# A new beginning for a fused attention and FFN kernel: the order of its first loads, and the norm of tiles 8 to 31 turned to columns by DMA transposes

## The reference

```
normed = (x - mean) * rsqrt(var + 1e-5) * g + b
v, gate = split(silu(normed @ W_h + b_h))            # 2048 columns each
qk = silu(normed @ W_qk + b_qk)                      # 128 columns
quad_q, lin_q, quad_k, lin_k = qk * gamma[h] + beta[h]
per group of 256 tokens: attn = relu(quad_q @ quad_k.T / 256 + bias)**2
quad_out = attn @ v ;  lin_out = lin_q @ (sum over all tokens of lin_k.T @ v / 4096)
y = layernorm(x + (gate * (quad_out + lin_out)) @ W_o + b_o + x)
out = layernorm(y + relu(y @ W1 + b1) @ W2 + b2)
```

## Time and profile before

| | us |
|---|---|
| median of 3 runs | 1748.19 (1748.16 to 1748.96) |
| the profiled execution, its own time | 1749.52 |
| its span, core 0, first to last instruction | 1748.0 (other cores 1745.3 to 1747.4) |
| PE busy | 1703.2 |
| DVE, ACT, POOL busy | 548.0, 436.3, 316.4 |
| mean granted TensorE clock, core 0 | 0.994 |

### The profile page before, as it was taken

How to read it: one execution, slowest core, us unless ns; L and a number is a source line. 1 busy time by engine, 2 the same in 40 slices (tenths; PEclk the granted TensorE clock), 3 DMA queues, 4 the chain that set the end, 5 groups by cost and what they waited for, 6 DMA issues and landing times.

```text
span 1748.0 us, 23816 instructions; the slowest of 8 cores (1745.3 to 1748.0 us)
## 1 busy us (share of the span) xinstructions
PE 1703.2 (97%) x8320; PEld 805.3 (46%) x8320; DVE 548.0 (31%) x947; ACT 436.3 (25%) x684; POOL 316.4 (18%) x494
## 2 busy tenths in 40 slices
PE   3899999999999999999999999999999999999998
PEld 1344444445445445445444444444444444444443
DVE  3466654354454454454302012020120211202102
ACT  2344444312212213213230311303113022040220
POOL 3444442022322322312301001010010000100001
PEclk9899999999999999999999999999999999999999
DMA  7857762637467477454870112012220121110201
GB/s 176 181 141 187 190 166 79 175 112 155 141 164 152 143 169 144 144 139 123 191 217 37 61 37 84 12 44 67 37 63 22 49 73 37 50 36 25 73 1 48
DMA packets 93523, 180.94 MB, mean 104 GB/s; under 512 B 39648, under 2 KB 43744, under 8 KB 93408
## 3 DMA queue, kind: packets, MB, share of 16 engines
q1 hardware_dynamic: 78288, 149.77, 27.0%
q0 software_dynamic: 15120, 29.63, 12.5%
HBM read 139.53 MB, written 69.47 MB: 120 GB/s over the span
## 4 chain that ended last, share of the span: by engine, by line
PE 96%; DMA 1%; DVE 1%; POOL 1%; issue 1%; ACT 0%; SPq 0%; POOLq 0%; DVEq 0%; ACTq 0%
PE pb L725 25%; PE pb L702 25%; PE pb L668 13%; PE pb L634 13%; PE pb L569 12%; PE pb L656 3%; PE pb L650 2%; PE pb L579 2%; DMA xs<-x 1%; PE pb L539 1%; PE pb L550 1%; POOL n0s L451 0%; DVE nfm L815 0%; DVE bnst L227 0%; DVE bnst L228 0%
## 5 line engine op out<-in xcount | busy, mean ns | idle before, releaser
L702 PE MATMUL pb<-xfm,w1s 128*128 128x512 bf16 x2048 | 443.3, 379 | 0.0
L796 ACT ACTIVATE h<-pb,prms 128x512 bf16<-128x512 f32 x256 | 175.9, 687 | 653.2 <-PE pb L702 653.2
L702 PEld LDWEIGHTS pb<-xfm,w1s 128*128 128x128 bf16 x2048 | 200.4, 98 | 241.6
L929 DVE TENSOR_TENSOR xr<-pb,xr 128x512 f32<-128x512 f32 x64 | 44.2, 691 | 715.4 <-PE pb L725 715.4
L569 PE MATMUL pb<-wvs,nfm 128*128 128x512 bf16 x1024 | 248.8, 387 | 0.1
L634 PE MATMUL pb<-nfm,wgs 128*128 128x512 bf16 x1024 | 240.6, 379 | 0.0
L725 PE MATMUL pb<-w2a,h 128*128 128x512 bf16 x1024 | 231.5, 379 | 0.0
L668 PE MATMUL pb<-wos,gated 128*128 128x512 bf16 x1024 | 224.6, 379 | 0.0
L237 POOL TENSOR_SCALAR veps<-mv 128x1 f32<-128x1 f32 x96 | 21.8, 227 | 1002.2 <-DVE mv L232 1001.2
L725 PEld LDWEIGHTS pb<-w2a,h 128*128 128x128 bf16 x1024 | 100.2, 98 | 120.8
L569 PEld LDWEIGHTS pb<-wvs,nfm 128*128 128x128 bf16 x1024 | 100.3, 100 | 117.2 <-issue 12.9
(11 more groups left out here) (59 smaller groups left out, 1001.8 us busy)
## 6 DMA issues: line engine op xcount, KB each, us to landing
v_sp<-vst SPq DMA_DIRECT2D x32, 512.0 KB, 8.1
vb<-v_sp SPq DMA_DIRECT2D x32, 512.0 KB, 7.1
xr<-x SPq DMA_DIRECT2D x32, 512.0 KB, 13.1
x_sp<-xr SPq DMA_DIRECT2D x32, 512.0 KB, 3.0
xr<-x_sp SPq DMA_DIRECT2D x32, 512.0 KB, 8.0
out<-xr SPq DMA_DIRECT2D x32, 512.0 KB, 2.6
xt<-x SPq DMA_DIRECT2D x24, 512.0 KB, 5.7
w_sp<-w POOLq DMA_DIRECT2D x32, 256.0 KB, 13.8
```

The lines of the kernel that those rows point to most:

```text
L702: mm = te.matmul(pb[4 + n % 2][:], w1[:, w_:w_ + 128], xfm[:, x_:x_ + 512], start=(c == 0), stop=(c == 7))
L796: sc.activation(h1[:, ci * 512:(ci + 1) * 512], pb[4 + n % 2][:], AF.Relu, bias=prm[:, P_B1 + ci:P_B1 + ci + 1]).then_inc(S["s_h1"], 1)
```

## The change

First loads. SP issues x 0, x 1, prm (which now holds the identity as well), x 2, then Wv slice 0 as f32 in four parts of 512 KB into `wvf`, x 3, bv (now stored replicated for all partitions, in two parts), x 4, Wqk as f32 into `wqkf`, x 5 to x 7. ACT casts pieces 0 to 3 of slice 0 ahead of its first eviction, DVE pieces 4 to 7 behind its first. GpSimd loads slices 1 to 3 behind norm 2, 5 and 7. PE begins with 18 matmuls on zeros and has four more behind the transposes of tile 0.

Order. Units 4 to 11 alternate between slice 0 of tiles 4 to 7 and slice 1 of tiles 0 to 3. The statistics of tiles 3 to 7 stand at slots 0 to 4, those of a later tile at the slot of the columns of the tile before. Block 0's and block 1's qk stand at slots 5 and 11, their `lk_transpose` at 8 and 15, and GpSimd makes the heads of both behind norm 7.

Columns of tiles 8 to 31. PE's transposes and the evictions by ACT and DVE go. Instead SP issues a DMA transpose of the norm, SBUF to SBUF, for each tile (`columns`) at slots 14, 18, 22, 26, 30 and so on, and DVE applies g and b in place to the finished columns of a block (`affine`: eight operations of 128 x 512 bf16, four at slot 16b-3 and four at 16b-2). Norm t waits for the DMA transpose of tile t-2.

Smaller: GpSimd's -mean/std is split off `rs_chain` (`shift`) and left out in the last phase; bo and b2 are loaded from replicated arrays.

```diff
+GROUPS = ((0, 0), (1, 0), (0, 4), (1, 4), (2, 0), (2, 4), (3, 0), (3, 4))
+def place(u):
+    if 4 <= u < 12:
+        return 8 + (u - 4) // 2 - 4 * (u % 2)
+    return u
+def at_place(w):
+    if w < 32:
+        s, t0 = GROUPS[w // 4]
+        return t0 + w % 4, s
+    return w // 4, w % 4
...
+def store_slot(q):
+    return 13 if q == 1 else 4 * q + 5
 def t_slot(t):
     if t < 8:
-        return (0, 0, 0, 1, 2, 4, 5, 6)[t]
-    return 16 * (t // 4) - 15 + 4 * (t % 4)
+        return (0, 0, 1, 2, 3, 5, 7, 9)[t]
+    return 16 * (t // 4) - 18 + 4 * (t % 4)
 def stat_slot(t):
-    return (0, 1, 2, 3, 4, 8, 11, 14)[t - 3] if t < 11 else t_slot(t - 3)
+    return 4 + t if t < 11 else t_slot(t - 1)
+def aff_slot(b):
+    return 16 * b - 3
 def qk_slot(b):
-    return (3, 9)[b] if b < 2 else 16 * b
+    return (5, 11)[b] if b < 2 else 16 * b
 def lkt_slot(b):
-    return (7, 12)[b] if b < 2 else 16 * b + 4
+    return (8, 15)[b] if b < 2 else 16 * b + 4
...
# SP
         load_x_first(0)
+        load_x_first(1)
         sy.dma_start(out=prm[:], in_=prm_h[:, :]).then_inc(d_prm, 16)
-        sy.dma_start(out=ident[:], in_=id_h[:, :]).then_inc(d_id, 16)
-        load_x_first(1)
         load_x_first(2)
+        for c in range(4):
+            sy.dma_start(out=wvf[:, c * 1024:(c + 1) * 1024],
+                         in_=wv_h[0, :, c * 1024:(c + 1) * 1024]).then_inc(d_wvf[c], 16)
+        load_x_first(3)
         load_bv(0)
-        for t in range(3, 8):
+        load_x_first(4)
+        sy.dma_start(out=wqkf[:], in_=wqk_h[:, :]).then_inc(d_wqk, 16)
+        for t in range(5, 8):
             load_x_first(t)
+        load_bv(1)
...
+        def columns(t):
+            wt(sy, "s_n0", t + 1)
+            if t == 8:
+                wt(sy, "s_T", 8)
+            b, i = divmod(t, 4)
+            dst = nfm[:, b * 4096:(b + 1) * 4096].rearrange("p (c t) -> p c t", c=8)[:, :, i * 128:(i + 1) * 128]
+            sy.dma_start_transpose(out=dst, in_=n0_tile(t)).then_inc(d_T[t % 2], 16)
...
+        wt(sy, "s_n0", 6)
         load_x(8)
-        load_bv(1)
         load_x(9)
...
         for u in range(0, NU + 6):
-            for t in range(11, NT):
-                if ((10, 14)[t - 11] if t < 13 else t_slot(t - 5)) == u:
-                    load_x(t)
+            for t in range(8, NT):
+                if t_slot(t) == u:
+                    columns(t)
+                    if t + 3 < NT:
+                        load_x(t + 3)
...
# GpSimd
-        load_wv(0)
-        gp.dma_start(out=wqk[:], in_=wqk_h[:, :]).then_inc(d_wqk, 16)
...
             if t >= 10:
-                wt(gp, "s_T", t - 1)
+                wt(gp, d_T[t % 2], 16 * ((t - 8) // 2))
...
-            if t in (3, 5, 7):
-                load_wv((t - 1) // 2)
-            if t % 4 == 1 and t >= 5:
+            if t in (2, 5, 7):
+                load_wv(t // 2 if t < 7 else 3)
+            if t == 6:
+                head_lk(0)
+            if t == 7:
+                heads(0)
+                head_lk(1)
+                heads(1)
+            if t % 4 == 1 and t >= 13:
                 head_lk(t // 4 - 1)
-            if t % 4 == 1 and t >= 9 or t == 7:
-                heads(t // 4 - 1 if t > 7 else 0)
+                heads(t // 4 - 1)
...
# PE
+        def warm(n):
+            wt(te, "s_zero", 1)
+            for _ in range(n):
+                te.matmul(pb[3][:], vst[:, 0:128], vst[:, 128:640], start=True, stop=True)
...
         def v_unit(u):
...
             if s == 0:
-                wt(te, "s_nfa", t + 1)
-                wt(te, "s_nfd", t + 1)
+                wt(te, "s_nfa", min(t + 1, 8))
+                wt(te, "s_nfd", min(t + 1, 8))
+                wt(te, "s_aff", t // 4 - 1)
             wt(te, "s_vad", u - 1)
             for c in range(8):
+                if u == 0:
+                    wt(te, "s_wca", min(c + 1, 4))
+                    wt(te, "s_wcd", c - 3)
...
+        warm(18)
...
                 transposes(t)
+                if t == 0:
+                    warm(4)
...
# ACT
+        def cast_wv(c):
+            sc.wait_ge(d_wvf[c // 2], 16)
+            sc.copy(wv[:, c * 512:(c + 1) * 512], wvf[:, c * 512:(c + 1) * 512]).then_inc(S["s_wca"], 1)
+        for c in range(4):
+            cast_wv(c)
...
# DVE
+        def affine(b, half):
+            for i in range(2):
+                wt(ve, d_T[i], 16 * (2 * b - 2))
+            for c in range(4 * half, 4 * half + 4):
+                o_ = b * 4096 + c * 512
+                a = ve.tensor_scalar(nfm[:, o_:o_ + 512], nfm[:, o_:o_ + 512],
+                                     prm[:, P_NG + c:P_NG + c + 1], prm[:, P_NB + c:P_NB + c + 1],
+                                     ALU.mult, ALU.add)
+            if half:
+                a.then_inc(S["s_aff"], 1)
...
         for u in range(NU):
             for t in tiles_at(u):
                 nfm_evict(t)
-            for t in range(3, NT):
+                if t == 0:
+                    for c in range(4, 8):
+                        cast_wv(c)
+            if u < 5:
+                stats_a(u + 3)
+            for t in range(8, NT):
                 if stat_slot(t) == u:
                     stats_a(t)
+            for b in range(2, NB):
+                if u in (aff_slot(b), aff_slot(b) + 1):
+                    affine(b, u - aff_slot(b))
```

More of the change, by code:

```diff
@@ L73, in tiles_at @@
 def tiles_at(u):
-    return [t for t in range(NT) if t_slot(t) == u]
+    return [t for t in range(8) if t_slot(t) == u]
 def block_at(slot_of, u):
@@ L93, in build_program @@
     x_h = din("x", [NTOK, DM])
[L94 to L97, removed]
+    prm_h = din("prm", [128, P_N + 64])
+    bv_h = din("bv", [128, HID])
+    bo_h = din("bo", [128, DM])
+    b2_h = din("b2", [128, DM])
     wv_h = din("wv", [4, 128, 4096])
@@ L126, in build_program @@
     o = 131072
[L127 removed]
     biasT = at("biasT", o + 256, 512, F32)
[L129 removed]
+    prm = at("prms", o + 3072, P_N + 64, F32)
+    ident = prm[:, P_N:P_N + 64].bitcast(BF16)
     gs = at("gs", o + 2624, 4, F32)
@@ L447, in norm0 @@
             x_landed(gp, t)
+            shift(gp, t)
             wt(gp, "s_nm", t + 1)
             if t >= 10:
-                wt(gp, "s_T", t - 1)
-            gp.tensor_scalar(n0_tile(t), x_tile(t),
-                             rstd[:, j:j + 1], nmr[:, j:j + 1], ALU.mult, ALU.add).then_inc(S["s_n0"], 1)
+                wt(gp, d_T[t % 2], 16 * ((t - 8) // 2))
+            gp.tensor_scalar(n0_tile(t), x_tile(t), rstd[:, j:j + 1], nmr[:, j:j + 1],
+                             ALU.mult, ALU.add).then_inc(S["s_n0"], 1)
         def head_lk(b):
@@ L518, in emit_gpsimd @@
                 i = t % 4
+                if t >= 8:
+                    wt(gp, "s_x2f", t - 7)
+                shift(gp, NT + t)
                 if t == 0:
@@ L556, in lk_transpose @@
             for i in range(4):
-                mm = te.transpose(pT[:, i * 128:(i + 1) * 128], lkfm[:, i * 128:(i + 1) * 128], ident[:])
+                mm = te.transpose(pT[:, i * 128:(i + 1) * 128], lkfm[:, i * 128:(i + 1) * 128], ident)
             mm.then_inc(S["s_lkT"], 1)
@@ L748, in emit_scalar @@
                 wt(sc, "s_hd", b)
-                sc.activation(qkf[:], pb[7][:], AF.Silu, bias=prm[:, P_BQK:P_BQK + 1]).then_inc(S["s_qks"], 1)
-            q, j = divmod(u, 4)
+                sc.activation(qkf[:], pb[0 if b == 0 else 7][:], AF.Silu, bias=prm[:, P_BQK:P_BQK + 1]).then_inc(S["s_qks"], 1)
+            q, j = divmod(place(u), 4)
             if j == 0 and q >= 3:
@@ L833, in attn, with cast_wv @@
             ve.scalar_tensor_tensor(attnT[:, a_:a_ + 512], sims[:], 0.0, sims[:], ALU.max, ALU.mult).then_inc(S["s_att"], 1)
-        for t in range(3):
-            stats_a(t)
-            if t == 0:
-                scale_heads()
+        def cast_wv(c):
+            ve.wait_ge(d_wvf[c // 2], 16)
+            ve.tensor_copy(wv[:, c * 512:(c + 1) * 512], wvf[:, c * 512:(c + 1) * 512]).then_inc(S["s_wcd"], 1)
+        ve.memset(vst[:, 0:640], 0.0).then_inc(S["s_zero"], 1)
+        stats_a(0)
+        stats_a(1)
+        scale_heads()
+        stats_a(2)
         for u in range(NU):
@@ L1006 @@
         a["L0_ffn_b1"].reshape(32, 128).T,
+        np.eye(128, dtype=ml_dtypes.bfloat16).view(np.float32),
     ], axis=1)
```

106 lines of the change are left out of this document (59 added, 47 removed).

## The result

The changed kernel takes 1735.09 us (median of 4 runs, 1734.67 to 1738.21), the one before 1748.18 (1748.04 to 1748.96) in the same session: ratio 0.9928, 95% interval 0.9911 to 0.9945. That is 13.1 us faster, where the prediction said 28.2. The range (1709 to 1738) holds it only because its upper end was set past rival B; the gain itself missed by 15.1 us. In some executions the cores of one die show a lower granted clock and the time is longer; every time given here is a median of the other executions.

A forecast was written before the change was run, and what follows sets the result against it. PE, busy 97%, was taken to bound the kernel, so only its idle or half-speed stretches and work taken off it count: 22.6 + 10.6 - 3 - 2 = 28.2 us from 1749.5 gives 1721.3, so 1720 for the median; range 1709 to 1738.

The forecast's parts named there:

- rival B: Blocks' columns: they land late in each block, 3 us over the need x 6 = 18 instead of 2; 1736, chance 0.12.
- Transposes off PE: Tiles 8 to 31: 24 transposes of 0.44 us leave PE, with no stall hiding them; gain 10.6 us.
- The beginning: Up to V unit 21: the new load order cuts the loss from 47.6 to 25 us; gain 22.6, bounds 15.6 and 30.
- I take 25: New beginning: us still lost, a little over the sum of 22.5, since a first order loses something unseen.
- 0.36 MB/us: First loads on SP: assumed transfer rate, putting x 1 at 6.4 and Wv's four parts at 9.7 to 14.1 us.
- the 47.6 lost: Old beginning: V unit 21's start at 95.0 less 47.4 us of PE work done by then.
- x 5 after 32 us: Beginning: named sign that the forecast is wrong; x 5 was let land at 28 us.
- rival A: Beginning: bound by transfers, x 5 to x 7 and Wv slice 1 late; gain 11 instead of 22.6, 1732, chance 0.13.
- `affine`: 3 said: Slots 16b-2 of five blocks: DVE's added work stalls PE 0.4 to 1.4 us each, 2 to 7 in all, 3 taken.
- Lateness of the columns: 2 said: DMA transposes of six blocks: mostly no wait, 0 to 3 us each, 2 us taken in all.
- 7.2 us from issue, 8.5 to the need: Tile 4b+3's DMA transpose: lands 7.2 us after SP can issue it, while DVE needs it at 8.5.
- Rival C: SBUF transposes: one tile takes more than the 7.8 us four units leave, 23 us per us over; 1765, chance 0.10.

The follow-up runs named there:

- free_columns: Changed kernel with a 32-byte-a-partition copy in place of each DMA transpose, affine reading block 0, output wrong: 1726.27 us, 0.9873.
- pe_columns3: Changed kernel with columns of tiles 8 to 31 back on PE, ACT and DVE, block 0's qk waiting for its own four tiles: 1736.94 us, 0.9932.
- after: The changed kernel itself, against the kernel before: 1735.09 us, 0.9928; run again in another session 1739.93, 0.995.
- plain_copy: Changed kernel with each DMA transpose replaced by an untransposed copy of the same bytes in 256-byte pieces, output wrong: 1727.21 us, 0.9879.
- wv1_behind_3: Changed kernel with the casting load of Wv slice 1 behind norm 3 instead of norm 2: 1736.97 us, 0.9935.
- plain_loads: Changed kernel with Wg and Wo casting loads from tile 15 on, plus eight unused plain 512 KB loads behind norms 8 to 15: 1742.67 us, 0.9961.
- affine_later: Changed kernel with affine one slot later, at 16b-2 and 16b-1: 1749.83 us, 1.0005.

## Why the prediction was wrong

The runs split the change: 1748.2 before; 1736.9 with the new beginning alone; 1726.3 with columns for free; 1735.1 with the real transposes (from three groups, the middle two known to about 3 us by their intervals). So -11.3, -10.7 and +8.8 in place of -22.6, -10.6 + 3 and +2 (3 being `affine`, 2 the late DMAs).

**Transposes off PE: right.** 10.6 said, 10.7 measured with `affine` included. The traces agree: from V unit 21 to stage 2 the mean core takes 229.9 us before and 220.6 in `free_columns`, 9.3 less for 22 of the 24 tiles, 9.7 by the prediction's 0.44.

**The beginning: the step that failed.** "I take 25" for what the beginning loses; by the prediction's own count (the work done by unit 21 is 0.9 less) it lost 78.7 - 46.5 = 32.2 us on the mean core, from 93.6 - 47.4 = 46.2: 14.0 gained at that point, 11.3 at the end in `pe_columns3`. Two inputs were off. First, the rate: 0.36 MB/us was read from the slices from 17.5 us on in the earlier trace rows, and the slow stretch ahead of them was put down wholly to GpSimd's casting loads. In after GpSimd issues its first load at 15.36 us. GB/s in 40 slices, 0 to 20 us, of after:

```profile
GB/s 0 0 0 0 82 164 287 369 287 229 172 115 163 284 303 254 333 270 172 147 180 221 238 328 352 336 352 295 287 246 303 336 311 336 393 442 426 377 393 270
```

And the windows: two of after, then one of before (the last two columns are DMA share and GB/s):

```profile
5.00:15.00 10.00, 5.16 (x24) 2.00 (x22) 5.96 (x21) 1.41 (x3) 6.34 (x12) 0.96 0.98 252
5.00:18.70 13.70, 6.33 (x33) 2.99 (x32) 6.72 (x23) 3.75 (x9) 8.01 (x14) 0.84 0.98 283
```

```profile
5.00:15.00 10.00, 1.01 (x8) 0.78 (x8) 1.92 (x11) 1.50 (x4) 2.24 (x4) 1.00 0.96 160
```

So without the casting loads the stretch is faster, 252 GB/s instead of 160, but with engines as full it still dips (115 near 5.5 us, 147 near 9.5) and isn't at 360. x 1 came 2.9 us after x 0 and x 2 3.0 after that, 0.17 MB/us; x 1 to the last part of Wv, 3 MB, took 18.7 - 5.0 = 13.7 us, 0.22 MB/us. In these 13.7 us the engines moved 3.9 million bytes, and these six transfers are 3.15 million, so some 0.7 million belonged to others, most likely to those issued behind Wv, while the prediction let each transfer have the whole rate in turn. Second, the 47.6 lost was core 0's, the slowest; the mean core had 1.4 less to win. What follows unit 0 is a chain of DVE work with transfers in it: DVE stands in order, waits 2.77 us for x 4 until 29.05 and 1.21 for x 5 until 33.45 (28 said, and "x 5 after 32 us" was named as a sign of wrong); norm 4 then holds unit 3 to 34.36, and unit 4 starts at 38.11 (31.5 said). Later slice 1, an earlier bias and a warm PE, one at a time, took away 1.8 us or nothing. The gain is rival A's number, 11; its cause, late transfers, is seen in these waits, but no run with faster transfers shows how much of the loss is theirs and how much is DVE's own chain.

**`affine`: 3 said, at most 0.8 on a core.** Four take 1.38 us, inside the 1.1 to 1.65 set; what failed is the step from there to a stall of PE. In `free_columns`, which keeps all of them, PE has no wait of over 0.4 us between unit 21 and stage 2 on four cores and a single one of 0.4 to 0.8 on the other four.

**Lateness of the columns: 2 said, 8.8 measured.** The step "7.2 us from issue, 8.5 to the need" holds for the median (7.3). What it lacked is the pair of late landing and held issue: tile 9 landed after 18.7 us, SP's next issue, taken for 1.1 to 4.5 us at most, was 12.0, and the transposes behind it in the order left late. Rival B had late columns in all six blocks at 3 us each; they came in two blocks, at up to 8.7 us in block 2 on some cores and not on others, and at 1.5 to 2.9 us in block 3 on all. That 1735 nearly meets B's 1736 is chance: most of the miss is the beginning's. A mean over cores shows half of it: stage 2 starts at 304.4 us on the mean core of after and at 310.4 on the slowest; with free columns at 299.1 on the mean core. The prediction counted on one core. So the miss of 15.1 is 11.3 from the beginning and 6.8 from the lateness, less 3 for `affine`.

**Rival C: false.** A transpose takes 1.7 us to issue (median) and lands in 7.3, under the 7.8 that four units leave. How long it holds the DMA engines follows from the DMA share of 150 to 230 us, in after and in `free_columns`, both on core 2:

```profile
150.00:230.00 80.00, 80.00 (x381) 36.53 (x380) 46.49 (x88) 25.89 (x42) 38.00 (x65) 1.00 0.96 213
```

```profile
150.00:230.00 80.00, 79.63 (x371) 36.35 (x377) 46.43 (x90) 25.87 (x41) 36.89 (x62) 1.00 0.76 186
```

(0.96 - 0.76) x 80 us over the 80 / 7.76 = 10.3 tiles is 1.6 us of all 16 engines a tile, eight squares of 128 x 128; with the means of the eight cores (0.97 and 0.76) it is the same. The plain copy of the same bytes, with 0.88, holds them for 0.9 us. The Trainium skill ("VectorE: DVE Perf Modes", The three transpose paths) has 1309 ns for one square, an estimated 10.5 us for eight in a row. The 1.6 us of engine time and the median landing of 7.3 don't bear that out. The Trainium skill ("Advanced Engine Details and Errata", X-Bar Transpose) has transposes as fast as ordinary DMAs. In the median landing that agrees (`plain_copy` 7.3 as well); in the time of the engines (1.6 against 0.9 us) and of the issue (1.7 against 0.6) it doesn't.

**Open.** Why the same program is late on one core and not on the next, and on other cores in the next execution; why tile 9's transpose lands so late beside other loads, and whether SP's long issue really waits for that landing, as the order of events suggests; why the first loads run at 0.17 to 0.22 MB/us; and how much of `wv1_behind_3`'s 1.8 us is lost to the columns' lateness, which grew on its slowest core, and how much to chance.

## What to carry to other kernels

Give a DMA that stands in an in-order queue a slack from its worst issue and landing beside the other queues' traffic, not from its median; three slots more of lead and no casting loads beside the first block's transposes made the change worth 22 us here instead of 13. One late landing there can hold the queue for everything behind it, so look at the issue times of the queue as well as at the landings. On eight cores count with the slowest: a wait that strikes one core at random costs as if it struck all. Read the rate of first loads from the first microseconds of the trace, not from where the queue has come up to speed, and don't give the neighbour the whole of a dip unless a row without the neighbour shows it gone: here taking the casting loads away brought 252 GB/s, not the 360 counted on.

## What was not expected of the hardware

- The issue of a DMA transpose on SP, 1.7 us in the median, took up to 12.0 us beside casting loads on GpSimd's queue and up to 10.4 beside plain ones (`plain_loads`); a plain copy of the same bytes never took more than 1.6. In after the long issues ended when the transpose ahead had landed (-0.2 to +2.9 us).
- In 4 us of that stretch the DMA engines of core 2 show a share of 1.58 and move 37 GB/s:

```profile
80.00:84.00 4.00, 4.00 (x20) 1.84 (x19) 2.86 (x6) 1.26 (x2) 1.06 (x3) 1.00 1.58 37
```

- x 1 and x 2 arrive at 0.17 MB/us with nothing on GpSimd's queue, and the row of GB/s dips to 115 there; in the slices from 16.5 to 19.0 us it has 336 to 442.
- A wait of PE costs more than itself: after 7.63 us of idling (after, core 2) the next unit took 3.25 us instead of 1.89, with a granted clock of 0.50 from 104 to 108 us; after 2.45 us (`affine_later`, core 4) qk and the next unit took 1.7 us more, with 0.61 from 145 to 148. After a wait of 1.71 us (after, core 2, at 93.36) the next unit took 1.89, the full clock.
